# A halo copy moved to ScalarE, and the sixteen states of a scan divided anew among the engines

## What is computed

```python
xz = x @ in_proj_w.T                      # 1024 channels of x_in, 1024 of z
x_in = silu(causal_conv4(x_in) + conv_b)  # depthwise, 4 taps along time
x_dbl = x_in @ x_proj_w.T                 # dt_raw, B (16 states), C (16 states)
dt = clip(softplus(dt_raw @ dt_proj_w.T + b), 1e-4, 10)
# for each of 16 states n, along time:
h_n = h_n * exp(dt * A_n) + dt * B_n * x_in
y = sum_n h_n * C_n
```

## Time and profile before

| what | value |
|---|---|
| median of three runs | 4980.63 us (4979.41 to 4981.1) |
| the profiled execution | 4978.69 us, of which the profile's span is 4976.9 us |
| TensorE, VectorE busy over the span | 4217.4 us (85%), 3526.9 us (71%) |
| GpSimd, ScalarE busy over the span | 2654.5 us (53%), 2218.5 us (45%) |
| inner_stage | about 2159 to 2580 us of the span |
| scan_stage | about 2586 to 4105 us of the span |

### The profile page before, as it was taken

The page is one execution under the profiler, slowest core; times in us unless marked ns, Lnnn a source line. Parts: engine busy times, 40 slices in busy tenths (PEclk is TensorE's granted clock), DMA queues, the critical chain, the costliest instruction groups (busy, mean ns, idle before and its releaser), DMA issues. The chain is left out here.

```text
span 4976.9 us, 49426 instructions
## 1 busy us (share of the span) xinstructions
PE 4217.4 (85%) x16117; PEld 2401.9 (48%) x16117; DVE 3526.9 (71%) x3880; ACT 2218.5 (45%) x3950; POOL 2654.5 (53%) x1555
## 2 busy tenths in 40 slices
PE   8997987599999459979837988888888888978886
PEld 6776875344444124433314555555555543435553
DVE  5554337522277555559978999999999997955676
ACT  1211114322255631037755676666766664423442
POOL 4544965100033011118868999999999986622221
PEclk9998996599999779989969999999999999989998
DMA  3332233242278765425453242242242217630100
GB/s 106 105 95 63 79 100 118 76 155 87 101 280 299 290 265 203 152 96 196 162 191 118 70 133 100 70 142 91 71 157 75 70 41 268 228 115 18 34 26 34
DMA packets 364162, 632.15 MB, mean 127 GB/s; under 512 B 67478, under 2 KB 153271, under 8 KB 351746
## 3 DMA queue, kind: packets, MB, share of 16 engines
q1 hardware_dynamic: 326850, 585.97, 33.7%
q10 hardware_dynamic: 37056, 43.00, 2.4%
HBM read 400.73 MB, written 228.15 MB: 126 GB/s over the span
## 5 line engine op out<-in xcount | busy, mean ns | idle before, releaser
L2255 POOL TENSOR_TENSOR sc_X<-sc_Bm,sc_w 128x1024 f32<-128x1024 f32 x512 | 1192.3, 2364 | 101.4 <-DVE sc_A L2431 42.1
L2379 PE MATMUL sc_yp<-sc_Z,sc_idn 128*128 128x512 f32 x1408 | 674.5, 602 | 23.2 <-DVE sc_Z L2436 21.4
L1329 PE MATMUL ff_ps<-ffn_R 128*128 128x512 f32 x1536 | 660.6, 592 | 0.7 <-issue 0.7
L2277 ACT ACTIVATE sc_A<-sc_dt,keep_A 128x1024 f32<-128x1024 f32 x512 | 575.2, 1123 | 162.4 <-DVE sc_Z L2436 84.2
L1329 PEld LDWEIGHTS ff_ps<-ffn_R 128*128 128x128 f32 x1536 | 291.2, 190 | 364.5 <-issue 363.8
L2307 ACT ACTIVATE sc_hT<-sc_tp,sc_ct 128x128 f32<-128x128 f32 x1280 | 362.8, 366 | 173.2 <-PE sc_tp L2359 172.2
L2379 PEld LDWEIGHTS sc_yp<-sc_Z,sc_idn 128*128 128x128 f32 x1408 | 248.5, 191 | 272.9 <-issue 209.1
L2366 PEld LDWEIGHTS sc_yp<-sc_idn,sc_hT 128*128 128x128 f32 x2560 | 306.6, 192 | 113.3 <-ACT sc_hT L2307 80.9
L2366 PE MATMUL sc_yp<-sc_idn,sc_hT 128*128 128x128 f32 x2560 | 318.1, 278 | 15.7 <-ACT sc_hT L2307 15.7
L2436 DVE TENSOR_TENSOR sc_Z<-sc_A,sc_Cm 128x1024 f32<-128x1024 f32 x256 | 313.5, 1225 | 8.9
L2431 DVE TENSOR_TENSOR_SCAN sc_A<-sc_A,sc_X 128x1024 f32<-128x1024 f32 x128 | 292.1, 2282 | 31.7 <-ACT sc_A L2277 28.9
(11 more groups left out here) (379 smaller groups left out, 8083.0 us busy)
## 6 DMA issues: line engine op xcount, KB each, us to landing
sc_Bm<-d_xd SPq DMA_DIRECT2D x64, 512.0 KB, 7.5
ffn_gate_d<-ff_o SPq DMA_DIRECT2D x96, 256.0 KB, 2.2
ffn_up_d<-ff_o SPq DMA_DIRECT2D x96, 256.0 KB, 6.3
ffn_g_d<-ff_z SPq DMA_DIRECT2D x24, 1024.0 KB, 6.7
ffn_R<-ffn_g_d SPq DMA_DIRECT2D x8, 3072.0 KB, 11.0
ffn_R<-ffn_up_d SPq DMA_DIRECT2D x8, 3072.0 KB, 21.6
ffn_R<-ffn_up_d SPq DMA_DIRECT2D x23, 1024.0 KB, 12.8
sc_Cm<-d_xd SPq DMA_DIRECT2D x44, 512.0 KB, 8.2
```

What stands on the lines that cost most here:

```text
L1329: last = nc.tensor.matmul(ps[:, 2 + t % 6], w[:, k, h * P:(h + 1) * P], xt[:, n, k], start=(k == 0), stop=(k == KD - 1))
L2255: nc.gpsimd.tensor_tensor(X[:, k % RX], Bm[:, n], w[:, j % 2], ALU.mult).then_inc(db, 1)
L2277: nc.scalar.activation(A[:, k % 2], dt[:, j % 2], ACT.Exp, scale=keepA[:, n:n + 1]).then_inc(ex, 1)
L2379: last = nc.tensor.matmul(yp[:, e * TB:(e + 1) * TB], idn[:], Z[:, zed(k) % RZ, e * TB:(e + 1) * TB], start=(n == FIRST), stop=(n == NS - 1))
```

## The change

The halo is copied by ScalarE, at the end of the round ahead, behind the last `copy_xi`; VectorE keeps the memset of round 4. In the scan stage the states are divided anew: turned 0, 2, 5, 8, 10, 12 (six, before 0, 3, 6, 9, 12), GpSimd 3, 7, 11 (before 4, 7, 10), VectorE 1, 4, 6, 9, 13, 14, 15 (seven, before eight: 1, 2, 5, 8, 11, 13, 14, 15). `hT` has two buffers, so a turned state's copies wait for the fold of the turned state two back. A product's slot in Z follows from its state alone (10 products a row in 4 slots). C is loaded spread over all partitions for 10 states instead of 11.

```diff
+            def copy_halo(n):
+                act.wait_ge(rev, 1 + n * RG)
+                act.wait_ge(cv, 1 + (n - 1) * CB)
+                nc.scalar.copy(xi[:, n % 2, :, 0:3], xi[:, (n - 1) % 2, :, TB:TB + 3]).then_inc(halo, 1)
...
                     if n < NB:
                         copy_xi(n, c)
+                    if c == CB - 1 and n + 1 < NB and n + 1 != NB // B:
+                        copy_halo(n + 1)
...
-                if n:
+                if n == NB // B:
                     dve.wait_ge(cv, 1 + (n - 1) * CB)
-                if n == NB // B:
                     nc.vector.memset(xi[:, n % 2, :, 0:3], 0.0).then_inc(halo, 1)
-                elif n:
-                    nc.vector.tensor_copy(xi[:, n % 2, :, 0:3], xi[:, (n - 1) % 2, :, TB:TB + 3]).then_inc(halo, 1)
...
-ON_POOL = (4, 7, 10)
-ON_PE = (0, 3, 6, 9, 12)
+ON_POOL = (3, 7, 11)
+ON_PE = (0, 2, 5, 8, 10, 12)
...
-        hT = s.sb("hT", [P, TQ, P])
+        hT = s.sb("hT", [P, 2, TQ, P])
...
-        def last_turned(k):
-            same = [m for m in ON_PE if m < k % NS]
-            return k // NS * NS + same[-1] if same else (k // NS - 1) * NS + ON_PE[-1]
+        def turned_two_back(k):
+            p = ON_PE.index(k % NS) - 2
+            return (k // NS + p // NE) * NS + ON_PE[p]
...
         def same_z(k):
-            zs = [m for m in range(NS) if not on_pe(m)]
-            p = zs.index(k % NS) - RZ
-            return (k // NS + p // NZ) * NS + zs[p % NZ]
+            users = [m for m in range(NS) if not on_pe(m) and zed(m) % RZ == zed(k % NS) % RZ]
+            p = users.index(k % NS) - 1
+            return (k // NS + p // len(users)) * NS + users[p]
...
-                if turned(k):
-                    act.wait_ge(mm, 1 + NS + added(last_turned(k)))
+                if turned(k) > 1:
+                    act.wait_ge(mm, 1 + NS + added(turned_two_back(k)))
```

More of the change, by code:

```diff
@@ L2260, in outputs @@
                 pool.wait_ge(cc[ci(n)], 1 + (i + 1) * 16)
-                pool.wait_ge(mm, 1 + NS + (added(same_z(k)) if zed(k) >= RZ else 0))
-                nc.gpsimd.tensor_tensor(Z[:, zed(k) % RZ], H[:, slot(n)], Cm[:, ci(n)], ALU.mult).then_inc(cp, 1)
+                pool.wait_ge(mm, 1 + NS + (added(same_z(k)) if same_z(k) >= 0 else 0))
+                nc.gpsimd.tensor_tensor(Z[:, zed(n) % RZ], H[:, slot(n)], Cm[:, ci(n)], ALU.mult).then_inc(cp, 1)
             for k in range(NU_):
@@ L2306, in turn @@
                     q = h * (TQ // 2) + b
-                    nc.scalar.activation(hT[:, q], tp[:, b * P:(b + 1) * P], ACT.Copy, scale=ct[:, i % 2, q, n:n + 1]).then_inc(tc, 1)
+                    nc.scalar.activation(hT[:, turned(k) % 2, q], tp[:, b * P:(b + 1) * P], ACT.Copy, scale=ct[:, i % 2, q, n:n + 1]).then_inc(tc, 1)
             def store(j):
@@ L2365, in fold @@
                 for b in range(TQ):
-                    last = nc.tensor.matmul(yp[:, b * P:(b + 1) * P], hT[:, b], idn[:], start=False, stop=False)
+                    last = nc.tensor.matmul(yp[:, b * P:(b + 1) * P], hT[:, turned(k) % 2, b], idn[:], start=False, stop=False)
                 last.then_inc(mm, 1)
@@ L2378, in add @@
                 for e in range(TC // TB):
-                    last = nc.tensor.matmul(yp[:, e * TB:(e + 1) * TB], idn[:], Z[:, zed(k) % RZ, e * TB:(e + 1) * TB], start=(n == FIRST), stop=(n == NS - 1))
+                    last = nc.tensor.matmul(yp[:, e * TB:(e + 1) * TB], idn[:], Z[:, zed(n) % RZ, e * TB:(e + 1) * TB], start=(n == FIRST), stop=(n == NS - 1))
                 last.then_inc(mm, 1)
@@ L2433, in _ @@
                         dve.wait_ge(sn, 1 + k + 1)
-                        dve.wait_ge(mm, 1 + NS + (added(same_z(k)) if zed(k) >= RZ else 0))
+                        dve.wait_ge(mm, 1 + NS + (added(same_z(k)) if same_z(k) >= 0 else 0))
                         dve.wait_ge(cc[ci(n)], 1 + (i + 1) * 16)
-                        nc.vector.tensor_tensor(Z[:, zed(k) % RZ], a, Cm[:, ci(n)], ALU.mult).then_inc(cd, 1)
+                        nc.vector.tensor_tensor(Z[:, zed(n) % RZ], a, Cm[:, ci(n)], ALU.mult).then_inc(cd, 1)
             with dve.If(clips == 1):
```

## The result

The changed kernel takes 4989.87 us (median of 17 runs, 4984.87 to 4994.9) against 4980.05 of the kernel before (median of 17, 4974.61 to 4985.87): a ratio of 1.002, with a 95% interval of 1.0013 to 1.0027. It is slower by 9.8 us, on the very edge of the 0.2% that the prediction took as its bound. The profiled execution took 4984.87 us, the fastest of its 17, with a span of 4983.1, 6.2 more than the one of before. The two parts of the change do nearly cancel, as forecast.

A forecast was written before the change was run, and what follows sets the result against it. VectorE was taken to lead both stages before; afterwards a 47.0 us chain of hand-overs sets the scan rows. 4978.69 - 28 (inner) + 30 (scan) = 4980.7 profiled, 4983 as median; forecast's own range 4968 to 4996, wider 4952 to 5005.

The forecast's parts named there:

- The row as a chain: Scan stage: hand-overs from one add(15) to the next sum to a 47.0 us row, +30 us in all.
- Half-way: Scan-stage rival: one there-and-back drops out as copies overlap TensorE's adds, row 46.2, total 4958; chance 0.10.
- VectorE waits before scan 2: Scan-stage sign: VectorE idle 2 to 3 us before scan 2 of each row, released by ScalarE's decay.
- Changes of chunk: Scan stage, first to last store: 4.5 us beyond the rows' own sum, kept unchanged after the change.
- Inner stage: Inner stage with the halo copy off VectorE: -28 us, range -33 to -20.
- 28, as TensorE starts with a lead: Inner stage: 28 us chosen between VectorE's 32.6 and the 24 to 21 if VectorE meets TensorE's rounds.
- The moved copy: Inner stage: six halo copies on ScalarE cost 0 to 3 us behind TensorE's transposes, counted as 0.5.
- Opening: Scan stage's opening: one C load less of 27 helps by up to 2 us; counted as 0.
- VectorE stays the bound: Scan-stage rival: ScalarE and TensorE hide the turns; -28 - 48 = -76, total 4904; chance 0.13.
- ScalarE takes the chain: Scan-stage rival: ScalarE, ready only 0.2 us early for state 10's second half, becomes late; row 47.6, total 5002; chance 0.17.
- The halo's cover only changes places: Inner-stage rival: VectorE's time becomes waits for TensorE's projections, rounds 44 us or more, only 8 won, 5003; chance 0.05.
- the margin is nil: Scan stage, kernel before, at the store: scan 2 starts right behind decay(2), so whatever delays add(15) against VectorE stops VectorE.

The follow-up runs named there:

- scan part alone: The changed kernel with the halo copy put back on VectorE, so only the scan stage differs from the kernel before: 5010.4 us, ratio 1.0054.
- product cut: The changed kernel with VectorE's product of state 6 by C cut to one column of 1024 from the second row on: 4990.16 us.
- x_dbl halved: The changed kernel with x_dbl summed over four of the eight channel groups on TensorE: 4970.91 us.
- the kernel with gates and store moved: The changed kernel with z projections in steps 0 to 3, 7, 10, 11, 12, z copies in 5 and 13, store behind decay 2: 4905.41 us.
- the halo copy alone: The kernel before with only the halo copy moved to ScalarE: 4963.83 us, ratio 0.9965.
- the five turned states with the later store: The kernel before, its scan division kept, with the halo copy on ScalarE and the store behind decay 2: 4963.15 us.

## Why the prediction was right, and where not

The forecast, 4983 for 4989.87 measured, lay in the right case by its own steps: two large parts that nearly cancel. The scan part alone came out at +30.1 for the +30 forecast. The inner part was mis-sized. In the two traces the terms add up: inner stage +7.4 against the forecast, opening -2.0, rows +2.5, changes of chunk -4.0, together +3.9. The forecast for the profiled execution, with the rows' 30.4 not rounded, was 4981.1, and it took 4984.87, 3.8 more. That the smaller terms take back half of the inner part's miss is luck. The median of the changed kernel lies 5 us above its profiled execution, which the forecast could not know.

- **The row as a chain: right, step by step.** The forecast's pieces, read off the row above: add 15 to scan 2, 4.59 (4.6 forecast); three scans and a product, 7.95 (7.9); ScalarE to fold 2, 2.98 (3.0); fold 2 to state 5's second half, 5.76 (5.7); that half, 1.84 (1.8); fold 5 to state 8's second half, 7.48 (7.4); that half, 1.88 (1.8); to state 10's second half, 3.11 (3.1); that half, 1.93 (1.8); to add 15, 9.63 (9.6). The sum is 47.15 where 47.0 had been laid out: the three there-and-backs took 5.65 instead of 5.4, and folds and adds behind a wait the rest. Over 31 rows, 15 at 47.13 and 16 at 47.03 make +32.9 over before, where +30.4 stood. "Half-way", a row of 46.2, did not come: all three there-and-backs are in the chain.
- **VectorE waits before scan 2: right**, 1.90 and 1.62 us, somewhat under the "2 to 3" since 1.05 of its slack went to scan 12 in chunks 0 and 2. That wait had been given as 0.7, covered by the slack; it was.
- **Changes of chunk: 4.5 us kept, 0.5 found.** 15 x 47.13 + 16 x 47.03 is 1459.4 of the 1459.9 measured. That is 4 us in the change's favour. Three other kernels with the same rows (scan part only, product cut, x_dbl halved) have 2.5, 1.5 and 2.7 us over their rows. That a VectorE with 2 to 3 us of slack a row absorbs what held it up before would be one explanation, but the kernel with gates and store moved, whose VectorE has no slack, has only 0.4. So why they cost less is open; all that is shown is that five turned states paid 3.9 to 9.0 us, and the change's six (0, 2, 5, 8, 10, 12) 0.4 to 2.7 in eight kernels.
- **Inner stage: -28 forecast, -20.6 measured.** This term fails by size. The bounds named were VectorE's 41.7 a round (-32.6) and TensorE's 43.35 to 44.1 (-24 to -21); "28, as TensorE starts with a lead" was the step that failed. No lead lasts: in rounds 2, 3 and 6, of 44.2 us, TensorE never waits for a silu; in rounds 4 and 5, of 43.0 and 43.2, it and VectorE each wait once for the other. The halved x_dbl shows that TensorE's work is on that path. The range's end of -20 had the profiled execution, but not the six traces in which the stage gives 17, nor the halo copy alone at -16.5 in the median. The rounds of "41.7 to 43.5" that were to show the forecast right did not come either: three reach 44.2.
- **The moved copy: 0.5 us forecast within 0 to 3, about 1 found.** It stands on ScalarE ahead of what TensorE's transposes wait for. With it their wait is 1.93 us, in round 4, which has the memset, 1.69. In rounds 2, 3, 6 and 7 TensorE has no later wait that hides this, so four times 0.24 us are on its path; in round 5 the 1.88 us for the silu hide it. The two lines of TensorE, rounds 3 and 4:

```profile
2277.20 1.29 PE L1706 MATMUL in_ps<-in_idn,in_x 128*128 128x128 f32 x8 [1.93 <-ACT in_xt L1762]
...
2321.18 1.14 PE L1706 MATMUL in_ps<-in_idn,in_x 128*128 128x128 f32 x8 [1.69 <-ACT in_xt L1762]
```

- **Opening: 0 forecast, -2.0 found** (first store 22.6 earlier, stage 20.6). The bound named held it. It need not be the change's doing: from the stage's first instruction to the first store there are 82.4 us before and 80.4 after, but 82.7, 80.7 and 82.4 in the other three kernels with the same scan stage. That it is the C load was not tried.
- **The rivals.** "VectorE stays the bound" fell with the product cut: 0.83 us less work a row (0.92 in chunks 1 and 3) changed nothing. But its own number, rows of 44.0 and 44.9, is what the kernel with gates and store moved reaches (43.88 and 44.85), so the sums were right and only the order stood in their way. The Trainium skill (Perfetto Trace Analysis, "Engine Utilization") says that in a well-optimized kernel at least one engine should approach full use. VectorE at 93% in chunk 0 (219.72 of 235.68 us over five rows) would have passed for it, and yet the row lost another 3.3 us there without any work removed; it took the idle that is left, and what releases it, to see the ring. "ScalarE takes the chain" did not come, but by little: ScalarE's copies of state 10's second half follow its z copy without a pause and start 0.68 us behind the transposes' start, where those of states 8 and 12, which ScalarE waits for, start 0.63 behind. The 0.2 us in hand that the prediction gave it were not there. "The halo's cover only changes places" spoke of rounds of 44 us and more and a gain of 8: three rounds did reach 44.2, but the gain was 17 to 20 us, since rounds of 47 to 49 stood there before.
- **The halo copy's price.** The Trainium skill (SBUF — State Buffer, "Who interferes with whom") gives the pair of ports that VectorE shares with GpSimd as "an exclusive lock" and ScalarE ports of its own. The 0.22 us of the same copy on ScalarE, with GpSimd busy beside it (3.00 of 3.00 us from 2274 to 2277), agrees. The prediction's estimate by that rule, 8 us for six copies that each wait for one GpSimd instruction, does not hold: the six took 41.2 us, and the move gave 17 to 20 us in the stage.

**One reading of before was carried too far:** "the margin is nil" at the store. As a reading it stands: VectorE comes to scan 2 without a wait, 0.06 us behind the end of decay 2. But a margin of nil is not yet a wait, and the five turned states with the later store show that the store bound nothing there. It was the six-state order that made the same 4.6 us from add 15 to scan 2 part of a ring. The forecast had that right, since the ring was laid out in full; the expectation for the later kernel, which looked for a wait before scan 2, had not, and missed.

## What to carry to other kernels

Where several engines run written-out lists and their sums a row lie within a tenth of each other (here 44, 44 and 40 us), lay out the ring of hand-overs once round before trusting any engine's sum. Here it gave the row to 0.13 us, and it also names the cheapest cure: a call moved by one step gave 58 us, work removed from the busiest engine gave none. Before an instruction is moved in such a list, follow what its operands' loads stand behind on the DMA-issuing queue, at the changes of chunk and in the first row as well as in the steady state. And when a bound is taken off one engine, count on the next engine's measured round, not on a mean of the two.

## What was not expected of the hardware

- A 24-element copy within SBUF takes 0.22 us on ScalarE in all six places (216 to 221 ns), where on VectorE, beside back-to-back GpSimd instructions, the same copy took up to 9.01 us. The first of VectorE's six, in round 1, took 0.17 us.
- TensorE's granted clock is below its full 2.4 GHz at the start of most inner rounds. In the changed kernel the window 2274 to 2285 has a granted clock of 0.69, within it 2279 to 2282 one of 0.50, the lower level of 1.2 GHz, and the first eight projection matmuls took 6.53 us; from 2286 to 2317 it is 1.00, and eight take 3.70:

```profile
2274.00:2285.00 11.00, 8.15 (x23) 3.89 (x22) 8.18 (x12) 10.33 (x18) 11.00 (x13) 0.69 0.45 146
2279.00:2282.00 3.00, 2.83 (x4) 1.28 (x5) 2.89 (x5) 2.97 (x5) 3.00 (x5) 0.50 0.66 237
2286.00:2317.00 31.00, 31.00 (x72) 12.13 (x71) 29.82 (x40) 23.07 (x38) 25.96 (x27) 1.00 0.56 210
```

```profile
2292.61 3.70 PE L1714 MATMUL in_ps<-in_xt,in_win 128*128 128x512 f32 x8
```

  Before the clock falls TensorE waits for copies between its transposes (0.24 and 1.93 us). Round 5 has the same waits and keeps a clock of 1.00, so they alone do not decide it. With x_dbl halved the same eight took 6.71 and 6.78 us in rounds 2 and 3, and the mean clock of 2159 to 2593 was 0.84, against 0.85 to 0.87 in the ten kernels with all of x_dbl. The eight matmuls lose 2.8 us, but the round does not: round 5, whose eight took 3.70, then waits 1.88 us for the last silu and is only 1.0 us shorter than round 3 (43.2 for 44.2). No run here tried to win that back.
